# A fused AdaLN, selective-scan and mixture-of-experts kernel: the last four blocks of tokens scanned one at a time, and one common pace for the steps from slot 392 on

## The reference, cut to what matters

```python
mod = (_silu(c) @ wmod).reshape(4, 6, 1, -1)           # sa, ca, ga, sb, cb, gb
h = _layernorm(x) * (1 + ca) + sa
# selective scan:
val, gate = split(h @ W_in); val = silu(conv3(val))     # 512 channels
B, C = val @ W_B, val @ W_C                              # 16 states each
Delta = softplus((val @ W_delta + delta_base) @ W_tau)
dA = Delta[..., None] * A
A_bar = exp(dA); B_bar = expm1(dA) / (dA + 1e-6) * Delta * B
h_t = A_bar_t * h_{t-1} + B_bar_t * val_t;  y_t = sum_n h_t * C_t
x = x + ga * ((y * silu(gate)) @ W_out + h)
# mixture of experts: 8 experts of hidden width 256, the best two per token, and a shared one
h = _layernorm(x) * (1 + cb) + sb
x = x + gb * (sum_e gate_e * (gelu(h @ W1_e + b1_e) @ W2_e + b2_e) + shared(h))
```

## Time and profile before

| what | value |
|---|---|
| median of 3 runs | 4584.77 us (4572.93 to 4586.28) |
| the profiled execution, its own time | 4587.09 us |
| its span in the trace | 4585.3 us |
| granted TensorE clock, mean | 0.899 |
| DVE busy | 4049.0 us (88%) |
| ACT busy | 3898.4 us (85%) |
| PE busy | 3873.8 us (84%) |
| POOL busy | 3534.7 us (77%) |

### The profile page before, as it was taken

How to read it: one execution, slowest core, us unless ns; L and a number is a source line. 1 busy time by engine, 2 the same in 40 slices (tenths; PEclk the granted TensorE clock), 3 DMA queues, 4 the chain that set the end, 5 groups by cost and what they waited for, 6 DMA issues and landing times.

```text
span 4585.3 us, 36853 instructions
## 1 busy us (share of the span) xinstructions
PE 3873.8 (84%) x9708; PEld 1612.3 (35%) x9708; DVE 4049.0 (88%) x3895; ACT 3898.4 (85%) x4226; POOL 3534.7 (77%) x2240
## 2 busy tenths in 40 slices
PE   8435436999989898998999998999989988989989
PEld 3111112333333333333333333333333333333444
DVE  2888899999999999999999999999999998889720
ACT  3988898989989898989989898989989898988811
POOL 0798987888889887888889787888888887868621
PEclk9667668999999999999999999999999998999989
DMA  5688877897888888898888888898888887756641
GB/s 183 187 259 260 253 219 215 241 270 221 256 250 236 251 235 245 241 268 226 256 247 239 254 239 241 242 271 225 259 242 243 238 232 189 203 159 192 167 136 51
DMA packets 352602, 1036.11 MB, mean 226 GB/s; under 512 B 41253, under 2 KB 44389, under 8 KB 345222
## 3 DMA queue, kind: packets, MB, share of 16 engines
q1 hardware_dynamic: 278666, 765.30, 48.4%
q0 software_dynamic: 73728, 268.47, 29.7%
HBM read 638.69 MB, written 126.51 MB: 167 GB/s over the span
## 4 chain that ended last, share of the span: by engine, by line
ACT 30%; PE 24%; issue 14%; DMA 12%; POOL 11%; DVE 9%; SPq 0%; POOLq 0%; DVEq 0%; ACTq 0%
DMA ysum<-hs 11%; PE ps L1115 8%; PE ps L1138 7%; ACT inv L703 5%; ACT th L714 4%; ACT abar L718 4%; ACT inv L696 4%; ACT inv L709 3%; PE ps L1080 3%; POOL inv L1389 3%; POOL hs L1362 3%; DVE ps L1178 2%; DVE ps L1184 2%; ACT L709 2%; DVE ps L1172 1%
## 5 line engine op out<-in xcount | busy, mean ns | idle before, releaser
L1389 POOL TENSOR_TENSOR inv<-inv,th 128x1024 f32<-128x1024 f32 x512 | 1264.0, 2469 | 190.7 <-ACT th L714 185.3
L1115 PE MATMUL ps<-hf,w1r 128*128 128x512 f32 x2304 | 1118.6, 638 | 79.3 <-ACT hid L820 48.1
L1362 POOL TENSOR_TENSOR hs<-hs,Cb 128x1024 f32<-128x1024 f32 x384 | 964.6, 2512 | 50.1 <-DVE hs L1202 33.4
L1172 DVE SCALAR_TENSOR_TENSOR ps<-ps,us 128x1024 f32<-128x1024 f32 x512 | 628.4, 1227 | 159.0 <-PE ps L1155 158.5
L1376 POOL DMA_DIRECT2D ysum<-hs x480 | 429.5, 895 | 409.8 <-DMA ysum<-hs 397.5
L1138 PE MATMUL ps<-w2r,hid 128*128 128x512 f32 x1584 | 726.6, 604 | 0.0
L696 ACT ACTIVATE inv<-delta,minus_pole 128x1024 f32<-128x1024 f32 (+1 forms) x640 | 576.8, 968 | 154.7 <-DVE ps L1184 154.6
L1191 DVE SCALAR_TENSOR_TENSOR ps<-delta,minus_pole,ps 128x1024 f32<-128x1024 f32 (+1 forms) x640 | 675.1, 1073 | 15.7
L1115 PEld LDWEIGHTS ps<-hf,w1r 128*128 128x128 f32 x2304 | 452.5, 203 | 663.2 <-issue 570.4
L1155 PE MATMUL ps<-Brow,pick 48*128 48x512 bf16 x1024 | 335.1, 410 | 413.2 <-DVE hs L1202 412.7
L1202 DVE TENSOR_TENSOR_SCAN hs<-abar,carry,ps 128x512 f32<-128x512 f32 (+1 forms) x384 | 683.5, 1801 | 0.3
(11 more groups left out here) (165 smaller groups left out, 4939.5 us busy)
## 6 DMA issues: line engine op xcount, KB each, us to landing
ysum<-hs POOLq DMA_DIRECT2D x512, 512.0 KB, 5.6
Cb<-c_rows SPq DMA_DIRECT2D x384, 512.0 KB, 4.5
w1r<-in_W SPq DMA_DIRECT2D x144, 512.0 KB, 5.4
w2r<-w_scaled SPq DMA_DIRECT2D x129, 512.0 KB, 8.0
Cb<-c_rows SPq DMA_DIRECT2D x128, 256.0 KB, 4.6
gbc<-expert_gates SPq DMA_DIRECT2D x128, 256.0 KB, 5.0
xa<-in_x SPq DMA_DIRECT2D x32, 512.0 KB, 6.8
aw<-in_W_val SPq DMA_DIRECT2D x64, 256.0 KB, 6.4
```

The lines of the kernel that those rows point to most:

```text
L1115: mm = t.matmul(o, w1r[:, n % 2, k, h * P:(h + 1) * P], hf[:, k, :], start=(k == 0), stop=(k == G - 1))
L1362: gp_.tensor_tensor(hs[:, c % 4, :], hs[:, c % 4, :], Cb[:, c % 2, :], ALU.mult).then_inc(hC_done, 1)
L1389: gp_.tensor_tensor(inv[:, c % 6, :], inv[:, c % 6, :], th[:, c % 3, :], ALU.mult).then_inc(thinv_done, 1)
```

## The change

`SIZES` gives the last four blocks (12 to 15) groups of their own, where before only blocks 14 and 15 had them. Slots 384 to 447 thus change from the paired to the single form. `LAST`, the slot and step from which `begins_at` places the steps, moves from 448 to 392, and the 152 steps 392 to 543 are spread over the 120 slots 392 to 511 (1.27 steps a slot on average). Each step's share of this time is now computed: 1.5, plus 4 if it is step 14 of its window, plus the costs of its PE jobs after `PE_COST`. The tail (slots 512 to 575) is as it was.

```diff
-        SIZES = [1, 1] + [2] * 6 + [1, 1]
+        SIZES = [1, 1] + [2] * 5 + [1, 1, 1, 1]
...
-        PACE = [(-12, FRONT_FROM, FRONT_AT, FRONT_AT), (2 * WIN, (NQ - 2) * WIN, 2 * WIN, (NQ - 2) * WIN), ((NQ - 2) * WIN, NQ * WIN, (NQ - 2) * WIN, (NQ + 1) * WIN), (NQ * WIN, (NQ + 2) * WIN, (NQ + 1) * WIN, (NQ + 3) * WIN)]
+        PACE = [(-12, FRONT_FROM, FRONT_AT, FRONT_AT), (2 * WIN, (NQ - 4) * WIN + 8, 2 * WIN, (NQ - 4) * WIN + 8), ((NQ - 4) * WIN + 8, NQ * WIN, (NQ - 4) * WIN + 8, (NQ + 1) * WIN), (NQ * WIN, (NQ + 2) * WIN, (NQ + 1) * WIN, (NQ + 3) * WIN)]
...
-        LAST = (NQ - 2) * WIN
-        STEPS_11_31 = (3.6, 2.0, 10.6, 3.6, 8.2, 7.2, 7.2, 7.2, 3.6, 9.0, 5.4, 5.4, 9.0, 7.2, 3.6, 7.2, 5.4, 5.4, 5.4, 5.4, 1.0)
-        FIRST_STEPS = (4.8, 9.6, 9.6, 6.4, 6.4, 9.4, 9.4, 2.0, 3.0, 4.0, 4.0) + STEPS_11_31
-        STEP_TIME = (0.5, 0.5, 0.5, 0.5, 0.5, 9.4, 9.4, 6.4, 6.4, 6.4, 6.4) + STEPS_11_31
-        PART_TIME = [(FIRST_STEPS if v < WIN else STEP_TIME)[v % WIN] for v in range(3 * WIN)]
+        LAST = (NQ - 4) * WIN + 8
...
         def begins_at(v):
-            if v >= LAST + 3 * WIN:
+            if v >= (NQ + 1) * WIN:
                 return v - WIN
             i = int(v - LAST)
-            return LAST + (sum(PART_TIME[:i]) + (v - LAST - i) * PART_TIME[i]) / sum(PART_TIME) * 2 * WIN
+            return LAST + (sum(PART_TIME[:i]) + (v - LAST - i) * PART_TIME[i]) / sum(PART_TIME) * (NQ * WIN - LAST)
...
+        PART_TIME = [1.5 + (4 if n % WIN == 14 else 0) + sum(PE_COST[j[0]] for j in pe_jobs(*divmod(n, WIN))) for n in range(LAST, (NQ + 1) * WIN)]
...
-                        pe_in_pieces(pe, LAST, NQ * WIN, LAST, LAST + 3 * WIN, begins_at)
+                        pe_in_pieces(pe, LAST, NQ * WIN, LAST, (NQ + 1) * WIN, begins_at)
```

## The result

The changed kernel takes 4623.85 us (median of 4 runs, 4621.49 to 4632.19); the kernel before, with one more run beside it, 4578.85 us. The ratio is 1.0094 (95% interval 1.0079 to 1.0109): about 43 us slower, where 12 us less were forecast and 4602 us was the upper end of the range.

The account below looks back on a forecast made before the run. It took DVE to lead in slots 384 to 447 and PE to be late in 448 to 511. 60 x 8.63 + 68 x 8.50 = 1096 us against 1108, -12, gave 4573 us; range 4541 to 4602.

Parts of the forecast that it names:

- The engines' needs: Slots 384 to 511: busy time a slot of DVE, ACT and PE after the change, the largest ACT's 8.27 us.
- stage I: Slots 384 to 443, windows 12 and 13 with front part: 60 slots at 8.63 us, 518 us, giving back about 39.
- stage II: Slots 444 to 511, windows 14 to 16: 68 slots at 8.50 us, 578 us, winning about 51.
- From need to time: Stage I: ACT's need at a 96% busy share, 8.63 us a slot; stage II: DVE's need, idle time and stalls, 8.50.
- Rival (4): Stage I: ACT becomes the bound, table loads bunch, busy share 0.90; +21 us, 4606; chance 0.20.
- rival (3): Stage II: waits for PE were never a matter of pace; 8.75 us a slot, +5 us, no change; chance 0.23.
- the tighter step: Window 14, steps 7 to 10: 0.65 slot in place of 1.6; up to 8 us more waiting, taken as 0.
- rival (2): Both stages: ACT's buffers hide uneven batches, DVE's wait falls to the paired stage's; -40 us, 4545; chance 0.25.

Follow-up runs that it names:

- the fourth kernel: The changed kernel with 2 units more for each of steps 7 to 10 of window 14: 4654.39 us, ratio 1.0162.

## Why the prediction was wrong, point by point

**The engines' needs were right.** Forecast and measured busy time a slot: stage I ACT 8.27 and 495.45 / 60 = 8.26, DVE 8.03 and 8.02, PE 7.82 and 7.85; stage II DVE 7.91 and 7.88, ACT 7.72 and 7.70, PE 7.77 and 7.97 (the one that is off, by 0.2). The form's price for ACT, the closer steps and the extra table loads are all in these; slots 384 to 511 have 100 loads before and 106 after, where 101 and 107 were counted ahead. The two largest groups of table loads in stage I of the kernel after (count, busy us, mean ns, idle before) again have 1.28 us a load and 0.02 us of idle time ahead of one:

```profile
L705 ACT ACT_TABLE_LOAD x20 | 25.7, 1283 | 0.4
L699 ACT ACT_TABLE_LOAD x16 | 20.5, 1283 | 0.3
```

The drain that the Trainium skill (ScalarE: Activation LUTs, What ACT_TABLE_LOAD costs) adds to each switch does not show: the 106 loads of the two stages together have 1.8 us of idle time ahead of them.

**The step that failed is "From need to time".** It took an engine's share of busy time from a stretch where it led (ACT at 95.8%) or the idle time of another stage (DVE's 0.29 us) and added the stalls that the trace of before had. Stage I came out at 8.92 and not 8.63 us a slot (17 us), stage II at 9.02 and not 8.50 (35 us). Together that is the miss. It left out the waits that come from the places of the engines relative to each other. In stage I the old arrangement had one step a slot with its boundary on the slot's: a bank that PE fills is emptied by ACT and DVE at a place, in that slot or one of the next two, that is set once for each of the 32 steps. The paired stage ran at 96% of DVE with it, and no need of an engine shows it. At 1.09 steps a slot every step has another place in its slot, and the changed kernel with one step a slot again (the old pace in pieces) has 505.5 us there, with ACT busy 479 us of it (95%), so that the busy share held where the places were kept. Doubling five steps, or PE half a slot further ahead of DVE, costs 36 and 26 us in this stage, though an engine's busy time rises by at most 14 and 10 us. In stage II this cannot be the reason, as it was off the slots before too (1.5 steps a slot, now 1.40). There the term that failed is the 0.29 us of idle time, taken from a stage with one step a slot as what DVE has left wherever PE has room: PE's jobs were thinned from 7.8 to 7.0 units a slot, and DVE still idled 1.13 us a slot.

**Stage I, the trade of its parts.** I had +39 us, from the needs and a busy share. Measured: +26 us for the form (480.7 to 507.1) and +28 for the pace (507.1 to 535.3). Over both stages the pace's share is 14 us (1134.6 to 1148.4), as stage I took over work of stage II. The form's is mostly ACT's, shown by its merge at the old pace (24 of 27 us over 64 slots, 18 by the medians). The two are not independent: at the new pace the same merge gave only 7 us, and without ACT's price the pace costs 528.2 less 482.8 = 45 us. Rival (4) named stage I and ACT as its bound, and its 551 us for the stage lie as far above the measured 535 as the forecast's 518 lie below it; the stage did not reach the 9.1 us a slot from which it was to decide, and its mechanism does not carry more than the form's half.

**Stage II.** I had -51 us; it was -13. DVE waits 60.4 us for PE there, where I had said that under 35 shows the forecast right and 60 or more rival (3). Of the other signs, DVE was to be over 92% busy there and was at 87%. The thinning by a tenth (20.5 to 22.9 slots a window) took little out of the wait. How much of the 13 us it made at all is open: without it, the same slots took 618.0 us with the computed table in the paired form (8 less than before) and 630.8 with the old pace in pieces. That these waits are not a matter of the pace, as rival (3) has it, is supported by this number (its 595 us for the stage were still 18 too few); but the computed table and the smaller lag took 16 us from the wait and 14 from the last 64 slots of the kernel before, so a part of it is a matter of placement. What PE waits for, in window 14 and about it:

```profile
PE ps L1088 <- POOL xn L1432: 16.3, 1, 16.3
PE ps L1131 <- POOL hid L1440: 11.1, 1, 11.1
PE ps L1113 <- ACT xn L816: 7.6, 1, 7.6
```

The first is the tighter step that the prediction named: 16.3 against 9.8 us, inside the "up to 8 more" that it priced at 0; with 8 units more of room the wait fell by only 2 us, so what the tighter step costs was not measured. The second and third, a gated hidden tile from POOL and a bank from ACT, it did not have.

**The chances.** Rival (4) and a part of (3) made 0.21 for slower; both were sized from need, so none reached past 4606. The lower end of the range does not follow from its working either: rival (2) with both of its lower bounds gives 4545 and not 4541.

**What stays open.** Which of the steps' places in a slot makes ACT and DVE late for PE's banks, and so what makes the pace's 28 us of stage I and DVE's 60 us of waiting in stage II. It is not one of these alone: ACT's throughput (the merge gave 8 to 10 us), ACT's lag (0.0 is worse than 0.3), the evenness, DVE's lag (9 us of the kernel at best). ACT merged and DVE's lag of 0.3 together, which would take away both sources of the table above, is the rival that was not run. Nor was the choice of PE's banks changed, which `bank_held_to` makes from places counted in steps, in all kernels alike. That late banks stand behind the waits for PE is seen in the timeline; that they alone make the 28 us is argued and not shown. The 30 us that 8 units of room cost in the fourth kernel are not explained beyond this.

## What to carry to other kernels

Where every engine works through an order written out by hand, first add up each engine's need, but do not go from need to time by a busy share of another stage: ask which of the engines' places relative to each other the change leaves as they were. A rate of one step a slot fixed such places here; leaving it cost 30 us in 60 slots, some of them for work that moved there, where no engine was at its limit. When such a pace is changed, sum the result over all stages between which work moves, as one stage's loss is partly another's gain. And a cost that sits on a second engine (ScalarE here) can surface as a wait of a third for a second, as DVE's wait for PE's row did.

## What the runs showed that I had not expected

The hand-over is tighter than any busy share says: with ACT's doubled instructions taken away at the old pace, VectorE was busy 98.5% of 64 slots and waited 1.2 us for TensorE; with them, 22.1 us, though ACT was not named as what VectorE waits for. And PE half a slot further ahead of DVE, with no work added, cost 26 us in 60 slots.
